# First attention stage of a two-layer decoder on one core: probabilities without their zero blocks, weighting in row halves, and a chain that is one unit longer

## The reference, cut to what matters

```python
# x: 32 sequences of 64 tokens, 256 wide, f32; 16 heads of 128
def _L0_attn_ref(x, W_Q, W_K, W_V, W_O, b_Q, b_K, b_V, b_O):
    q = jnp.einsum('bpd,hde->bphe', x, W_Q) + b_Q
    k = jnp.einsum('bpd,hde->bphe', x, W_K) + b_K
    v = jnp.einsum('bpd,hde->bphe', x, W_V) + b_V
    scores = jnp.einsum('bqhe,bkhe->bhqk', q, k) / ATTN_SCALE
    scores = jnp.where(causal, scores, IGNORE)
    attn = jax.nn.softmax(scores, axis=-1)
    z = jnp.einsum('bkhe,bhqk->bqhe', v, attn)
    return jnp.einsum('bqhe,hed->bqd', z, W_O) + b_O
x = x + _L0_attn_ref(_layernorm(x, axis=-1), L0_attn_W_Q, ...)
# then cross attention, feed-forward, a second layer of the same three kinds
```

## Time and profile before

| what | us |
|---|---|
| median of 3 executions | 1765.09 (1760.82 to 1766.98) |
| the profiled execution | 1766.67, of which the span 1764.9 |
| PE busy over the span | 1597.0 |
| DVE, ACT, POOL busy | 1088.4, 863.5, 672.9 |
| projection of unit 0 starts | 27.22 |
| last add_out starts | 560.0 |

### The profile page before, as it was taken

One profiled execution on the slowest core, in us unless ns is written; L12 is line 12 of the kernel. 1 busy time (PEld: TensorE's weight loads), 2 busy tenths in 40 slices (PEclk: granted clock), 3 DMA queues, 4 the chain that ended last, 5 costly groups with the idle time before them and its releaser, 6 DMA issues. The chain is left out here.

```text
span 1764.9 us, 37020 instructions
## 1 busy us (share of the span) xinstructions
PE 1597.0 (90%) x14668; PEld 1288.6 (73%) x14668; DVE 1088.4 (62%) x1734; ACT 863.5 (49%) x1466; POOL 672.9 (38%) x527
## 2 busy tenths in 40 slices
PE   6999999999996887799999797999996898999998
PEld 4888888888885665687788564666664675888887
DVE  5777677676776887576332477999995565111111
ACT  3555555455453565555422346676672674222222
POOL 0121211211213562431422255999995430323232
PEclk9999999999998997899999798999998997999999
DMA  3011111111112200000102020000000900000000
GB/s 104 16 63 55 40 62 60 34 61 60 51 44 101 85 2 26 7 11 11 40 1 105 21 65 7 1 2 1 2 1 19 359 22 1 1 13 6 8 12 12
DMA packets 72351, 70.26 MB, mean 40 GB/s; under 512 B 24816, under 2 KB 64368, under 8 KB 71840
## 3 DMA queue, kind: packets, MB, share of 16 engines
q1 hardware_dynamic: 72224, 68.46, 12.1%
HBM read 46.03 MB, written 19.27 MB: 37 GB/s over the span
## 5 line engine op out<-in xcount | busy, mean ns | idle before, releaser
L655 POOL TENSOR_TENSOR s_w_parts<-s_w_raw,s_w_parts 128x768 fp32r<-128x768 f32 x15 | 27.8, 1854 | 402.9 <-ACT s_w_parts L605 402.9
L1477 DVE TENSOR_TENSOR s6f_hid<-s6f_act_sb,s6f_u_ps 128x512 f32<-128x512 f32 x64 | 44.0, 688 | 219.3 <-PE s6f_u_ps L1428 219.3
L1500 POOL TENSOR_TENSOR s6f_hid_parts<-s6f_hid,s6f_hid_parts 128x512 fp32r<-128x512 f32 x64 | 82.8, 1294 | 225.8 <-ACT s6f_hid_parts L1466 225.8
L2216 POOL TENSOR_TENSOR s4b_with_q<-s4b_with_q 128x1024 f32<-128x1024 f32 x64 | 150.8, 2376 | 0.9 <-DVE s4b_with_q L2171 0.9
L2171 DVE TENSOR_TENSOR s4b_with_q<-s4b_c_ps,s_q_rows 128x2048 f32<-128x2048 f32 x64 | 146.0, 2284 | 2.2 <-PE s4b_c_ps L2310 2.2
L588 PE MATMUL s_o_ps<-s_w_parts,s_zT 128*128 128x256 f32 x768 | 110.8, 295 | 4.1 <-DVE x_rows L691 4.1
L529 PE MATMUL s_v_ps<-s_wv_parts,s_xnT 128*128 128x256 f32 x768 | 104.9, 287 | 8.2 <-ACT s_v L634 6.8
L1466 ACT ACTIVATE s6f_hid_parts<-s6f_hid 128x512 fp32r<-128x512 f32 x64 | 40.5, 632 | 145.0 <-PE s6f_o_ps L1448 140.8
L529 PEld LDWEIGHTS s_v_ps<-s_wv_parts,s_xnT 128*128 128x128 f32 x768 | 97.3, 191 | 13.8 <-ACT s_v L634 10.0
L1448 PEld LDWEIGHTS s6f_o_ps<-s6w_parts,s6f_hid_parts 128*128 128x128 f32 x768 | 99.1, 188 | 6.6 <-issue 1.0
L588 PEld LDWEIGHTS s_o_ps<-s_w_parts,s_zT 128*128 128x128 f32 x768 | 97.5, 193 | 8.8 <-issue 4.5
(11 more groups left out here) (329 smaller groups left out, 4003.8 us busy)
## 6 DMA issues: line engine op xcount, KB each, us to landing
stored_weights<-s1q_halves SPq DMA_DIRECT2D x16, 768.0 KB, 3.7
s6w_parts<-stored_weights SPq DMA_DIRECT2D x32, 384.0 KB, 7.6
s1q_packed<-in_codes SPq DMA_DIRECT2D x8, 384.0 KB, 4.4
s1q_scale<-in_scale_rows SPq DMA_DIRECT2D x8, 384.0 KB, 4.9
s3p_raw<-in_ffn_pieces SPq DMA_DIRECT2D x8, 384.0 KB, 8.7
early_values<-s_vbd SPq DMA_DIRECT2D x1, 2176.0 KB, 12.3
s_vbd<-early_values SPq DMA_DIRECT2D x4, 544.0 KB, 7.5
x_rows<-in_x SPq DMA_DIRECT2D x4, 512.0 KB, 5.6
```

The lines of the kernel that those rows point to most:

```text
L655: nc.gpsimd.tensor_tensor(w_parts[:, slot, 1, :, :], w_raw[:, slot, :, :], w_parts[:, slot, 0, :, :], ALU.subtract).then_inc(w_low, 1)
L1477: nc.vector.tensor_tensor(hid[:, f % 2, :], act_sb[:, f % 2, :], u_ps[:, f % 2, :], ALU.mult) \
L1500: nc.gpsimd.tensor_tensor(hid_parts[:, f % 2, 1, :], hid[:, f % 2, :], hid_parts[:, f % 2, 0, :], ALU.subtract).then_inc(low_done, 1)
L2216: nc.gpsimd.tensor_tensor(with_q[:, half, :, 0, :, n_, :], with_q[:, half, :, 0, :, n_, :], with_q[:, half, :, 1, :, 1 - n_, :], op).then_ ...
```

## The change

The zero blocks go. Tiles are taken in pairs: `xnT` holds, for each pair, first the tokens of sequence b = 0 of both tiles and then those of b = 1, so that a values matmul gives the rows of both tiles for one b. `prob` is 128x256 (rows: b and token; columns: tile and key), double buffered, and needs no memset. Two transposes of 128x128, one for each pair, take the place of four; their result has the keys of the pair's two tiles in its upper and lower 64 rows. `weigh` uses the upper and lower 64 rows of the array for the two tiles: 8 matmuls of 64 rows, 128 weights wide and 64 columns, into two PSUM banks, in the place of 4 with 128 rows and 128 columns. Scores and transposed probabilities share one PSUM bank, which adds two waits. `turn` and `weigh` move to lag 5 and `output` to lag 6; the listed order changes on PE, ACT and DVE.

```diff
-            prob = room.sb("prob", [P, TG, P])
-            probT = room.sb("probT", [P, TG * P])
+            prob = room.sb("prob", [P, 2, TG, S])
+            probT = room.sb("probT", [P, TG * S])
...
-            s_ps = room.ps("s_ps", [P, 512])
-            pT_ps = room.ps("pT_ps", [P, 512])
-            z_ps = room.ps("z_ps", [P, 512])
+            sp_ps = room.ps("sp_ps", [P, 512])
+            s_ps, pT_ps = sp_ps[:, 0:TG * S], sp_ps[:, TG * S:2 * TG * S]
+            z_ps = room.ps("z_ps", [P, 2, 512])
...
                     wait(pe, masked, u)
+                    wait(pe, pT_out, u - 1)
...
                     wait(pe, pT_out, u)
-                    for t in range(TG):
-                        last = nc.tensor.transpose(pT_ps[:, t * P:(t + 1) * P], prob[:, t, :], core.c("ident"))
+
+                    pe.wait_ge(masked, min(u + 2, U) if isinstance(u, int) else u + 2)
+                    for pair in range(2):
+                        last = nc.tensor.transpose(pT_ps[:, pair * P:(pair + 1) * P],
+                                                   prob[:, k % 2, 2 * pair:2 * pair + 2, :].rearrange("p t s -> p (t s)"),
+                                                   core.c("ident"))
...
-                    for t in range(TG):
-                        last = nc.tensor.matmul(z_ps[:, t * P:(t + 1) * P], v[:, k % G, t, k // G, :],
-                                                probT[:, t * P:(t + 1) * P], start=True, stop=True)
+                    for pair in range(2):
+                        for b in range(2):
+                            for n in range(2):
+                                rows, at = slice(n * S, (n + 1) * S), pair * P + b * S
+                                last = nc.tensor.matmul(z_ps[:, n, at:at + S], v[rows, k % G, pair, b, k // G, :],
+                                                        probT[rows, at:at + S], start=True, stop=True)
...
-                run_steps(pe, U, [(project, 3), (turn, 4), (scores, 3), (output, 5), (weigh, 4)], unroll=8)
+                run_steps(pe, U, [(project, 3), (turn, 5), (output, 6), (scores, 3), (weigh, 5)], unroll=8)
...
-                run_steps(act, U, [(v_copy(0), 3), (q_copy, 3), (k_copy, 3), (v_copy(1), 3), (probT_copy, 4), (exponent, 3),
-                                   (z_high_part, 4), (split_high, 0), (deq.scalar, 4)], unroll=8)
+                run_steps(act, U, [(v_copy(0), 3), (q_copy, 3), (k_copy, 3), (v_copy(1), 3), (probT_copy, 5),
+                                   (z_high_part, 5), (exponent, 3), (split_high, 0), (deq.scalar, 4)], unroll=8)
...
-                nc.vector.memset(prob[:, :, :], 0.0).then_inc(zeroed, 1)
-                dve.wait_ge(zeroed, 1)
-
...
-                    for b in range(2):
-                        rows = slice(b * S, (b + 1) * S)
-                        last = nc.vector.tensor_tensor(prob[rows, :, b * S:(b + 1) * S], ex[rows, :, :],
-                                                       rs[rows, :].unsqueeze(2).to_broadcast([S, TG, S]), ALU.mult)
-                    last.then_inc(prob_done, 1)
-
-                run_steps(dve, U, [(shift, 3), (normalise, 3), (z_low_part, 4), (add_out, 5), (deq.vector, 3)],
+                    wait(dve, pT_full, u - 1)
+                    nc.vector.tensor_tensor(prob[:, k % 2, :, :], ex[:, :, :],
+                                            rs[:, :].unsqueeze(2).to_broadcast([P, TG, S]), ALU.mult) \
+                        .then_inc(prob_done, 1)
+
+                run_steps(dve, U, [(add_out, 6), (shift, 3), (z_low_part, 5), (normalise, 3), (deq.vector, 3)],
                           unroll=8)
```

More of the change, by code:

```diff
@@ L265, with split_tokens @@
 PARTS = ((0, 0), (0, 1), (1, 0))
-def split_tokens(core, parts, mv, factor, tag, column_step=1, beside=None, high_beside=None):
+def split_tokens(core, parts, mv, factor, tag, column_step=1, beside=None, high_beside=None, pairs=False):
     nc = core.nc
@@ L283, in rows, with place @@
         def rows(t):
+            if pairs:
+                return turned[:, t % 4, 0:D].rearrange("p (c b s) -> p c b s", c=NC, b=2)
             return turned[:, t % 4, 0:D].rearrange("p (c q) -> p c q", c=NC)
+        def place(part, t):
+            return parts[:, part, :, t // 2, :, t % 2, :] if pairs else parts[:, part, :, t, :]
         @block.vector
@@ L289, in low @@
                 dve.wait_ge(high_done, t + 1)
-                nc.vector.tensor_tensor(parts[:, 1, :, t, :], rows(t), parts[:, 0, :, t, :], ALU.subtract) \
+                nc.vector.tensor_tensor(place(1, t), rows(t), place(0, t), ALU.subtract) \
                     .then_inc(low_done, 1)
@@ L311, in _ @@
                 act.wait_ge(turned_done, t + 1)
-                nc.scalar.activation(parts[:, 0, :, t, :], rows(t), ACT.Copy).then_inc(high_done, 1)
+                nc.scalar.activation(place(0, t), rows(t), ACT.Copy).then_inc(high_done, 1)
                 if high_beside and t == 8:
@@ L406, in stage_L0_attention @@
         oroom = Room(nc, octx, "s1")
-        xnT = oroom.sb("xnT", [P, 2, NC, NT, P], F32R)
+        xnT = oroom.sb("xnT", [P, 2, NC, NT // 2, 2, 2, S], F32R)
         mv = oroom.sb("mv", [P, NT, 2])
@@ L471, in low_weights @@
                                     ALU.subtract).then_inc(wv_low, 1)
-        split_tokens(core, xnT, mv, rstd, "s1t", beside=low_weights, high_beside=high_weights)
+        split_tokens(core, xnT, mv, rstd, "s1t", pairs=True, beside=low_weights, high_beside=high_weights)
         with ExitStack() as ctx:
@@ L525, in values @@
                     for n in range(2):
-                        t = 2 * half + n
                         for c in range(NC):
@@ L529, in values @@
                                 last = nc.tensor.matmul(v_ps[:, n * 2 * E:(n + 1) * 2 * E],
-                                                        xnT[:, px, c, g * TG + t, :], wv_parts[:, pw, c, :, :],
+                                                        xnT[:, px, c, g * 2 + half, n, :, :].rearrange("p t s -> p (t s)"),
+                                                        wv_parts[:, pw, c, :, :],
                                                         start=(c == 0 and (px, pw) == PARTS[0]),
@@ L547, in project @@
                                 last = nc.tensor.matmul(ps[:, :], weights(slot, pw, m, c),
-                                                        xnT[:, px, c, g * TG:(g + 1) * TG, :],
+                                                        xnT[:, px, c, g * 2:g * 2 + 2, :, :, :]
+                                                        .rearrange("p a b t s -> p (a b t s)"),
                                                         start=(c == 0 and (pw, px) == PARTS[0]),
@@ L633, in part @@
                         act.wait_ge(v_full, u + k + half + 1)
-                        nc.scalar.activation(v[:, k, 2 * half:2 * half + 2, :, :],
-                                             v_ps[:, :].rearrange("p (t h e) -> p t h e", t=2, h=2), ACT.Copy) \
+                        nc.scalar.activation(v[:, k, half, :, :, :],
+                                             v_ps[:, :].rearrange("p (b h e) -> p b h e", b=2, h=2), ACT.Copy) \
                             .then_inc(v_out, 1)
@@ L642, in z_high_part @@
                     wait(act, o_full, u)
-                    nc.scalar.activation(zT[:, 0, :], z_ps[:, :], ACT.Identity, bias=bias[:, k // G, 2:3]) \
+                    nc.scalar.activation(zT[:, 0, :, :], z_ps[:, :, 0:2 * P], ACT.Identity, bias=bias[:, k // G, 2:3]) \
                         .then_inc(z_high, 1)
-                run_steps(act, U, [(v_copy(0), 3), (q_copy, 3), (k_copy, 3), (v_copy(1), 3), (probT_copy, 4), (exponent, 3),
-                                   (z_high_part, 4), (split_high, 0), (deq.scalar, 4)], unroll=8)
+                run_steps(act, U, [(v_copy(0), 3), (q_copy, 3), (k_copy, 3), (v_copy(1), 3), (probT_copy, 5),
+                                   (z_high_part, 5), (exponent, 3), (split_high, 0), (deq.scalar, 4)], unroll=8)
             @block.gpsimd
@@ L666, in _ @@
             def _(dve):
-                nc.vector.memset(prob[:, :, :], 0.0).then_inc(zeroed, 1)
-                dve.wait_ge(zeroed, 1)
                 def z_low_part(u, rnd, k):
                     dve.wait_ge(z_high, u + 1)
-                    nc.vector.scalar_tensor_tensor(out=zT[:, 1, :], in0=z_ps[:, :], scalar=bias[:, k // G, 2:3],
-                                                   in1=zT[:, 0, :], op0=ALU.add, op1=ALU.subtract).then_inc(z_low, 1)
+                    nc.vector.scalar_tensor_tensor(out=zT[:, 1, :, :], in0=z_ps[:, :, 0:2 * P], scalar=bias[:, k // G, 2:3],
+                                                   in1=zT[:, 0, :, :], op0=ALU.add, op1=ALU.subtract).then_inc(z_low, 1)
                 def shift(u, rnd, k):
```

12 lines of the change are left out of this document (6 added, 6 removed).

## The result

The changed kernel took 1775.6 us, median of 5 runs (1774.6 to 1781.1), where five runs of the kernel before lie between 1760.8 and 1767.0; the ratio of all these runs is 1.0071, with an interval of 1.0060 to 1.0082. By the medians it is slower by 10.5 us (0.6%). The forecast was 1774.4 us, and slower was its likeliest outcome.

What follows compares the result with a forecast made beforehand. PE was taken to set the pace, busy 62.4 of 65 us. From 1766.7 us, - 17.0 - 14.7 - 7.3 + 42.6 + 3.3 + 2.4 gives 1776.0; that execution being 1.6 above the median, 1774.4 us, range 1747 to 1798.

Steps and rivals of the forecast that it cites:

- PE's own work: PE in the loop: two fewer transposes save 17.0 us; the short steps' wait before the scores goes, 14.7 us.
- Two transposes: PE, each unit: two transposes in place of four save 0.27 us, 17.0 us over 64 units.
- Weigh: PE's weighing: no change, 0.8 to 0.9 us a unit as loads pair; bounds 0.41 and 1.76.
- The waits: PE waits behind late weight loads: 4.63 us by k = 0, 1.45 at k = 4; seven times, 42.6 us.
- The landing: ACT's split of the weights waits for their DMA, until 4.43 us after the output's end.
- The wait of before: PE's one old wait at k = 0, about 1.0 us in 8 units, is replaced: 7.3 us off.
- The drain: Stage's end: one dependent step longer, between nothing and 6.6 us; 3.3 us taken.
- The clock: Slow clock after the long wait at k = 0: two falls of 1.2 us, 2.4 us.
- the shorter waits: Rival: loop waits shorter, so faster, 1745 to 1757 us; deciding point 4.0 us in 8 units; chance 0.23.
- The paying halves: Rival: weighing by row halves takes 0.41 us, saving 13 us, 1761 us; chance 0.12.
- the unpaired loads: Rival: the weighing's half-row loads go one by one, 1.76 us a unit, 1808 us; chance 0.07.
- The slow clock in each round: Rival: clock falls each time, with more waits of ACT's queue, + 6 to + 20, 1780 to 1795 us; chance 0.12.

Runs made afterwards that it cites:

- e12: e7 with ACT's unpacking copies taken between the copy of the transposed probabilities and that of the weighed values, not after the exponent; 1738.1 us.
- e13: e7 with the data path of the kernel before (zero blocks, four transposes, full-row weighing, separate PSUM banks), keeping e7's chain and moves; 1746.5 us.
- e10: e7 with the weighing in full 128 rows, eight records for sixteen, leaving out the separation of a pair's tiles; 1734.8 us.
- e11: e7 with the loop over the two row halves outermost, so the halves no longer alternate; 1776.8 us.
- e1: The changed kernel with SP issuing the loads of W_Q, W_K, W_O and W_V ahead of its wait for the output; 1764.0 us.
- e9: The kernel before with only the unpacking split by phase, its later phases one step later on DVE and ACT; 1762.7 us.
- e5: The changed kernel with the whole unpacking of DVE and ACT one step later, the loads still behind the output; 1785.8 us.
- e7: The changed kernel with the four weight loads ahead of SP's wait and the later phases of the unpacking one step later; 1746.3 us.

## Why the prediction was right, and where it was not

The sign, the size and the mechanism hold, the size in part by luck. The chain was followed link by link, and its length came out at 15.97 us where 16.38 was forecast. Taking links away gave the time back: the loads 11.6 us, the order of DVE 7.4, all waits together (after against e12) 37.5. But the sum was right because errors of some 7 to 10 us in it cancel. Step by step, for the first stage:

- **PE's own work**: forecast - 31.7 us over 64 units; measured 4 x (9.16 - 9.00) + 4 x (6.79 - 6.26) = 2.76 in 8 units, - 22. The scores' wait went in full. **Two transposes** save 0.39 us from their start to the next work, not 0.27: 0.22 by their number, the rest because the output follows (e13). The output pass takes 1.60 us from start to start instead of 1.53, which was not foreseen either.
- **Weigh** was the mis-sized term: no change was forecast, 0.8 to 0.9 us; it takes 1.04, + 0.23 x 64 = 15 us. The loads did pair, as read from the earlier trace rows: sixteen take 0.97 us. But the row shows less than it seemed to: it is the head of a group of eight, cut off where its window ended, and all eight take 0.95 us there, beside matmuls of 384 columns. By the rule of columns that the prediction follows, taken alone, sixteen loads would be the 1.76 us of the upper bound, and not the 0.86 that the prediction gives for it; the 0.86 came of the pairing read from the row. What I did not see is that the weighing now follows the scores, which costs 0.10 (e10, e13), and that the halves cost 0.13 besides. The Trainium skill, "TensorEngine Tiling (Array Packing)", Key Properties, states that different tiles can load weights and run matmuls in parallel. This case's traces agree: 1.04 us against 1.53 when the halves don't alternate (e11). The same page of the Trainium skill, Theoretical Speedup, has up to 2x for a small contraction. It does not show here: the halves are slower than full rows (1.04 against 0.91).
- **The waits**: forecast 4.63 at k = 7 and 0, measured 1.49 + 2.26 = 3.75; forecast 1.45 at k = 4, measured 0.90. In the round shown that is 4.65, and 4.65 x 7 = 32.6 us, not 42.6; round by round the three distances exceed their usual ones by 30.4 us in all. The chain was only 0.4 us shorter; PE's own work beside it was longer, above all by the weighing, and that covers part of the chain. So the term that cost PE 15 us gave some of it back here.
- **The landing**: 4.25 us after the output's end, forecast 4.43. Its removal was put at 17 us among the rivals and measured 11.6 (e1), because the next link, DVE with the residual ahead of the shift, lies close behind: the wait for the values rose from 15.0 to 18.7 us in all, with a fall of the clock in every second round.
- **The wait of before**, 7.3 us, was taken off rightly, but in e9 its removal alone brought nothing: a new wait for Q took a part, and a store at the stage's end is next in line.
- **The drain**: forecast + 3.3 for a dependent step, measured 17.5 - 14.8 = 2.7, part of it slow clock.
- **The clock**: forecast two falls, 2.4 us, both behind the long wait at k = 0. There were three in the loop, behind stops of 2.23, 1.84 and 1.13 us, the last of them at k = 7. They cost 1.3, 1.2 and 1.5 us, 4.0 in all, by what the work behind them took longer.

The seven distances of 8 units after add up to 465.5 us, 38.2 more than the own work of 7 x 61.04. Of these 30.4 are the waits and 4.0 the clock; 3.8 are in pieces too small to assign. The sum of what was measured is - 22 - 7.3 + 38.2 + 2.7 = + 11.6, against + 10.2 at the end of the first stage; some 1 us stays unassigned.

Of the rivals, the shorter waits came nearest: the waits were a quarter shorter, yet PE's gain was smaller too, so the point below which it would have been faster beyond what a measurement can tell, 4.0 us in 8 units, had moved to 2.6 ((22 + 7.3 - 3.3 - 2.4 - 5.3) / 7). The 1745 us that this rival gives for "only one of them left" does not follow from its terms: without the 4.63 it is 1742, without the 1.45 it is 1764. The paying halves and the unpaired loads are excluded, the latter by e11, which shows what they cost. The slow clock in each round, with ACT's unpacking copies behind the load, did not happen in the changed kernel but did in e5, at 1785.8 us within the rival's 1780 to 1795.

## What to carry to other kernels

When a consumer is put one unit later in a software pipeline, look at every transfer that is released by it: the transfer moves by a unit too, while what needs it may not. Then read the queue behind that need on each engine in order, and ask of each move also what else falls in the same step: the same shift of the unpacking cost 10 us with late loads and gained 14 with early ones. Look at what follows a wait, too: in e5 the waits had hardly grown, but they had come together in one stop of 3 us, and the slow clock behind it made the loss. And split a change into its data path and its order before crediting either: here the order and the moves alone (e13) reach 1746.5 us, as with the new data path (e7), so the rearrangement of the chain carried the gain.
